# Softmax attention on TensorE: key tiles taken in pairs instead of singly

## The chip, the cores and the metric

One core of a Trainium2 chip runs the whole program. The metric is the device time of one execution in microseconds (us), as a median of several runs. TensorE multiplies, VectorE reduces, ScalarE exponentiates, GpSimd adds, SyncE issues most transfers.

## The reference

Four conditioned blocks follow each other on x of 2 x 2048 rows and 512 columns: a selective scan (Mamba), a softmax attention, and two linear attentions. The change lies in the second alone. Cut to what matters:

```python
def _L1_cond_ref(x, emb, src_mask, ...):
    xn = layer_norm(x, norm_w, norm_b)
    q = (xn @ q_w + q_b).reshape(Bx, Tx, H, -1)      # H = 16 heads of 32
    k = (xn @ k_w + k_b).reshape(Bx, Tx, H, -1)
    att = jnp.einsum('bnhl,bmhl->bnmh', q, k)
    att = att + (1.0 - mask) * -1000000.0
    att = jax.nn.softmax(att, axis=2)                # over the 2048 keys
    v = ((xn @ v_w + v_b) * src_mask[:, :, None]).reshape(Bx, Tx, H, -1)
    y = jnp.einsum('bnmh,bmhl->bnhl', att, v).reshape(Bx, Tx, Dx)
```

With two sequences and 16 heads there are 32 heads of 2048 queries by 2048 keys.

## The kernel before

`stage_attention` is written out by hand: each engine has its own program, the order in it is the order of execution, and engines wait for each other on counting semaphores. Every head is 16 **units** `u`, a unit being one tile of 128 keys against all 2048 queries in `QB` = 4 chunks of 512.

Queries and keys lie stacked (`q_st`, `k_st`; three slots, so three heads are in flight). Each score is computed twice. The **maximum** matmul (`max_mm`) puts 128 queries on the partitions and 512 keys along the bank; VectorE's `reduce` takes the row maximum out of one of three banks (`ps_max`, `BANKS` = 3), and a maximum matmul waits until the bank three items earlier is read (`free_bank`). When all 64 maxima of a head are there, VectorE makes one small tile `m_all`, TensorE turns it (`turn_max`), ScalarE and VectorE split it into two parts (`first_part`, `second_part`), and SyncE writes them as two rows into `q_st` (`max_rows`). The **score** matmul (`score_mm`) then puts 128 keys on the partitions, and the stacked rows subtract the maximum; ScalarE's `exp` empties one of three `ps_s` banks into `prob`, which has `SLOTS` = 4 units.

The **product** (`pv_mm`) multiplies the four chunks of `prob` with the values, as four tiles of 32 columns side by side; each of the four instructions leaves two records in the trace. GpSimd adds the `prob` of the units of a group (`SIZES`, six groups a head) into one of two `pair_sum` buffers, and the **denominator** (`den_mm`) multiplies that sum by ones, again in four column tiles. GpSimd may start a group only when the denominator of the group two earlier is done. `turn_o` turns the finished head's products and denominators back; VectorE's `read_o` inverts and multiplies them.

The maxima run ahead of the scores: during unit u of head hd TensorE makes the maxima of head hd + 1, `LEAD` = 3 units further on, and from unit `TURN_MAX` = 13 those of head hd + 2. During unit u it makes the scores of unit u + 1. `turn_o` follows unit 2, `turn_max` unit 13. The order of a unit on TensorE:

```python
for c in range(QB):
    if u + 1 < QT:
        score_mm(hd, u + 1, c)
    elif hd + 1 < HEADS:
        score_mm(hd + 1, 0, c)
    if tiles:
        max_mm(item_at(hd, "max", u, c), *tiles[c])
pv_mm(hd, u)
```

Of the kernel before, what the change touches and what calls it, by code (L numbers as in the profile page):

```python
# [952 lines left out]
QT = S // P  # L953
# [169 lines left out]
def stage_attention(nc, a, keep, parts, mask_parts, v):  # L1123

    with ExitStack() as ctx:
# [3 lines left out]
        QB = S // CH  # L1129
        NMAX = QT * QB  # L1130
        PER = NMAX // QT
        LEAD = 3
        SIZES = (2, 3, 3, 2, 3, 3)
        GROUPS = [tuple(range(sum(SIZES[:g]), sum(SIZES[:g + 1]))) for g in range(len(SIZES))]
        NGRP = len(GROUPS)
        GROUP_END = {units[-1]: g for g, units in enumerate(GROUPS)}
# [9 lines left out]
        SLOTS = 4  # L1146
        HEADS = NB * H1
        TURN_MAX = QT - LEAD
        TURN_O = 2
        DEN_LAG = 2  # L1150
        q_st = [r.sb(f"q_stack{i}", [ROWS, S], F32R) for i in range(3)]
        k_st = [r.sb(f"k_stack{i}", [ROWS, S], F32R) for i in range(3)]
        prob = [r.sb(f"prob{i}", [P, S]) for i in range(SLOTS)]
# [16 lines left out]
        s = {n: r.sem(n) for n in names.split()}  # L1170
# [4 lines left out]
        def max_tiles(hd, u):  # L1175

            ahead, i = (1, (u + LEAD) * PER) if u < TURN_MAX else (2, (u - TURN_MAX) * PER)
            return [(hd + ahead, i + j) for j in range(PER)] if hd + ahead < HEADS else []

        def bank_items(hd):  # L1180

            items = []
            for u in range(QT):
                items += [("max", u, j) for j in range(len(max_tiles(hd, u)))]
                if u == TURN_O and hd:
                    items.append(("turn_o", u, 0))
                if u == TURN_MAX and hd + 1 < HEADS:
                    items.append(("turn_max", u, 0))
            return items

        BEFORE = NMAX + 1 + LEAD * PER
# [4 lines left out]
        def item_at(hd, kind, u, j=0):  # L1196

            return first_item[hd] + bank_items(hd).index((kind, u, j))
# [57 lines left out]
        @block.tensor  # L1256
        def _(pe):
            def free_bank(seq):
                if seq >= BANKS:
                    pe.wait_ge(s["bank_read"], seq - BANKS + 1)  # L1260
                return ps_max[seq % BANKS]

            def max_mm(seq, hd, i):
                slot = hd % 3
                if i == 0:
                    pe.wait_ge(stack_in[slot], (hd // 3 + 1) * NSTACK * 16)
                qt, kc = divmod(i, QB)
                nc.tensor.matmul(free_bank(seq)[:, :], q_st[slot][0:ROWS_MAX, qt * P:(qt + 1) * P],  # L1268
                                 k_st[slot][0:ROWS_MAX, kc * CH:(kc + 1) * CH], start=True, stop=True).then_inc(s["bank_filled"], 1)

            def turn_max(seq, hd):
                pe.wait_ge(s["m_done"], hd + 1)
                nc.tensor.transpose(free_bank(seq)[0:QT, 0:P], m_all[:, :], keep["ident"][:, :]).then_inc(s["bank_filled"], 1)

            def turn_o(seq, hd):
                pe.wait_ge(s["o_copied"], hd + 1)
                bank = free_bank(seq)
                for t in range(CH // P):
                    mm = nc.tensor.transpose(bank[:, t * P:(t + 1) * P], o_raw[:, t * P:(t + 1) * P], keep["ident"][:, :])
                mm.then_inc(s["bank_filled"], 1)  # L1280
                pe.wait_ge(s["den_copied"], hd + 1)
                for t in range(CH // P):
                    mm = nc.tensor.transpose(ps_d[:, t * P:(t + 1) * P], d_raw[:, t * P:(t + 1) * P], keep["ident"][:, :])
                mm.then_inc(s["den_turned"], 1)

            def score_mm(hd, kt, c):
                n = (hd * QT + kt) * QB + c
                slot = hd % 3
                if kt == 0 and c == 0:
                    pe.wait_ge(s["max_in"], (hd + 1) * 32)  # L1290
                if n >= BANKS:
                    pe.wait_ge(s["exp_done"], n - BANKS + 1)
                nc.tensor.matmul(ps_s[n % BANKS][:, :], k_st[slot][0:ROWS, kt * P:(kt + 1) * P],  # L1293
                                 q_st[slot][0:ROWS, c * CH:(c + 1) * CH], start=True, stop=True).then_inc(s["s_mm"], 1)

            def pv_mm(hd, kt):

                if kt == 0:
                    pe.wait_ge(s["v_copied"], hd + 1)
                    if hd:  # L1300
                        pe.wait_ge(s["o_copied"], hd)
                pe.wait_ge(s["exp_done"], (hd * QT + kt + 1) * QB)
                for c in range(QB):
                    mm = nc.tensor.matmul(ps_o[c * DH1:(c + 1) * DH1, :], v_h[hd % 3][:, kt, :],  # L1304
                                          prob[kt % SLOTS][:, c * CH:(c + 1) * CH], start=(kt == 0), stop=(kt == QT - 1))
                mm.then_inc(s["o_mm"], 1)

            def den_mm(hd, g):

                if g == 0 and hd:  # L1310
                    pe.wait_ge(s["den_read"], hd)
                pe.wait_ge(s["sum_done"], hd * ADDS + sums[g])
                for c in range(QB):
                    mm = nc.tensor.matmul(ps_d[c * DH1:(c + 1) * DH1, :], ones[:, :],
                                          pair_sum[g % 2][:, c * CH:(c + 1) * CH], start=(g == 0), stop=(g == NGRP - 1))
                mm.then_inc(s["den_mm"], 1)

            for i in range(NMAX):
                max_mm(i, 0, i)
            turn_max(NMAX, 0)  # L1320
            for i in range(LEAD * PER):
                max_mm(NMAX + 1 + i, 1, i)
            for c in range(QB):
                score_mm(0, 0, c)
            pe.wait_ge(s["ones_set"], 1)
            for hd in range(HEADS):
                for u in range(QT):
                    tiles = max_tiles(hd, u)
                    for c in range(QB):
                        if u + 1 < QT:  # L1330
                            score_mm(hd, u + 1, c)
                        elif hd + 1 < HEADS:
                            score_mm(hd + 1, 0, c)
                        if tiles:
                            max_mm(item_at(hd, "max", u, c), *tiles[c])
                    pv_mm(hd, u)
                    if u >= DEN_LAG and u - DEN_LAG in GROUP_END:
                        den_mm(hd, GROUP_END[u - DEN_LAG])
                    elif u < DEN_LAG and hd and u - DEN_LAG + QT in GROUP_END:
                        den_mm(hd - 1, GROUP_END[u - DEN_LAG + QT])  # L1340
                    if u == TURN_O and hd:
                        turn_o(item_at(hd, "turn_o", u), hd - 1)
                    if u == TURN_MAX and hd + 1 < HEADS:
                        turn_max(item_at(hd, "turn_max", u), hd + 1)
            den_mm(HEADS - 1, NGRP - 1)
            turn_o(first_item[HEADS], HEADS - 1)

        @block.scalar
        def _(act):
# [23 lines left out]
                nc.scalar.activation(d_raw[:, :], ps_d[:, :], ACT.Copy).then_inc(s["den_copied"], 1)  # L1373

            first_part(NMAX, 0)
            for c in range(QB):
                exp(0, 0, c)
            for hd in range(HEADS):
                for u in range(QT):
                    for c in range(QB):  # L1380
                        if u + 1 < QT:
                            exp(hd, u + 1, c)
                        elif hd + 1 < HEADS:
                            exp(hd + 1, 0, c)
                    if u == TURN_O - 1 and hd:
                        copy_den(hd - 1)
                    if u == TURN_MAX and hd + 1 < HEADS:
                        first_part(item_at(hd, "turn_max", u), hd + 1)
                copy_o(hd)
            copy_den(HEADS - 1)  # L1390

# [1 line left out]
        def _(dve):  # L1393
# [16 lines left out]
            def read_o(seq, hd):  # L1410
                dve.wait_ge(s["den_turned"], hd + 1)
                if hd:
                    dve.wait_ge(s["bank_read"], item_at(hd, "turn_o", TURN_O) + 1)
                nc.vector.reciprocal(rden[:, :].rearrange("p (t c) -> p t c", c=QB),
                                     ps_d[:, :].rearrange("p (t c e) -> p t c e", c=QB, e=DH1)[:, :, :, 0]).then_inc(s["den_inv"], 1)
                dve.wait_ge(s["den_inv"], hd + 1)
# [13 lines left out]
            for i in range(LEAD * PER):  # L1430
                reduce(NMAX + 1 + i, 1, i)
            for hd in range(HEADS):
                for u in range(QT):
                    for j, tile in enumerate(max_tiles(hd, u)):
                        reduce(item_at(hd, "max", u, j), *tile)
                    if u == TURN_O and hd:
                        read_o(item_at(hd, "turn_o", u), hd - 1)
                    if u == TURN_MAX and hd + 1 < HEADS:
                        second_part(item_at(hd, "turn_max", u), hd + 1)
            read_o(first_item[HEADS], HEADS - 1)  # L1440


# [514 lines left out]
```

## Time and profile before

| | us |
|---|---|
| median of 3 runs | 5804.73 (5799.05 to 5807.38) |
| profiled execution, from its first to its last instruction | 5801.9 |
| first maximum matmul of the attention stage begins at | 2525.16 |
| last denominators of the stage begin at | 4347.55 |
| stretch 2632 to 4286: TensorE, VectorE, ScalarE, GpSimd busy | 1653.30, 1221.98, 1021.81, 1415.92 of 1654.00 |

The attention stage is nearly a third of the span. A row of the timeline gives the start, the duration, the engine, the line, the operation and how many were merged (x4); in brackets stands the idle time of the engine before it and what ended it. TensorE's weight loads have rows of their own (PEld). Matmuls overlap, and each lasts longer than the distance to the next: distances are read from starts. The first matmul after a wait or after a change of shape is recorded at its weight load, so the next one stands further away.

### The profile page before, as it was taken

The page shows a single profiled execution, that of the slowest core. Times are in us where ns is not written, and L with a number is a line of the kernel's source. Part 1 is how long each engine was busy: PE and PEld are TensorE (multiplying, and loading weights), DVE is VectorE, ACT ScalarE, POOL GpSimd, SP SyncE. Part 2 cuts the span into 40 slices and gives each one's busy share as a digit, 9 for nine tenths or more (in the row PEclk, how much of TensorE's full clock was granted, in tenths as well). Part 3 has the DMA queues.
Part 4 walks back from the last instruction along what each step waited for, and adds up shares of the span by engine and source line. Part 5 has one row for each costly group of instructions (what it writes and reads, how often), then busy time and mean ns, then how long its engine had stood idle before and what let it go on. Part 6 is the DMA issues. An engine that isn't in the chain of part 4 may idle for free. (4 is left out here: it accounts for less than half of the span.)

```text
span 5801.9 us, 58747 instructions
## 1 busy us (share of the span) xinstructions
PE 5279.5 (91%) x19584; PEld 2503.0 (43%) x19584; DVE 4122.6 (71%) x5430; ACT 2812.6 (48%) x4847; POOL 3279.8 (57%) x2136
## 2 busy tenths in 40 slices
PE   7888989888898879989999999999998889989898
PEld 2333333333333324445455454445544454544545
DVE  6999999999999963267777777777745444445444
ACT  4757566575756523326666666666661121312121
POOL 3879797887979741128888888888880000000000
PEclk9999999999999999979999999999999999999999
DMA  4021211212122023321111111111103202021101
GB/s 167 22 102 66 80 73 51 81 43 102 41 101 77 29 109 124 117 62 34 23 34 34 23 34 23 34 34 23 34 1 134 91 17 69 17 104 35 60 26 51
DMA packets 116735, 346.28 MB, mean 60 GB/s; under 512 B 12272, under 2 KB 13520, under 8 KB 102032
## 3 DMA queue, kind: packets, MB, share of 16 engines
q1 hardware_dynamic: 98512, 294.46, 15.5%
q0 software_dynamic: 9216, 33.56, 1.5%
q10 hardware_dynamic: 8704, 14.50, 0.7%
q8 instruction: 155, 2.54, 0.2%
q14 instruction: 148, 1.21, 0.1%
HBM read 274.29 MB, written 67.67 MB: 59 GB/s over the span
## 5 line engine op out<-in xcount | busy, mean ns | idle before, releaser
L1397 DVE TENSOR_REDUCE attn_mx<-attn_ps_max 128x1 f32<-128x512 f32 x2048 | 1270.1, 683 | 405.0 <-PE attn_ps_max L1268 400.4
L425 POOL TENSOR_TENSOR mamba_hc<-mamba_h,mamba_bc 128x1024 f32<-128x1024 f32 x512 | 1216.8, 2377 | 352.1 <-DVE mamba_h L658 298.2
L1363 ACT ACTIVATE attn_prob<-attn_ps_s 128x512 f32<-128x512 f32 x2048 | 1061.0, 604 | 590.3 <-PE attn_ps_s L1293 587.1
L805 PE MATMUL mamba_y<-mamba_hc,ident 128*128 128x512 f32 x2048 | 1013.0, 618 | 253.6 <-POOL mamba_hc L425 252.7
L1251 POOL TENSOR_TENSOR attn_pair_sum<-attn_prob 128x1024 f32<-128x1024 f32 x384 | 906.6, 2382 | 313.1 <-ACT attn_prob L1363 313.1
L528 ACT ACTIVATE mamba_da<-mamba_dt,mamba_a_neg 128x512 f32<-128x512 f32 x1024 | 689.6, 689 | 686.1 <-DVE mamba_h L658 682.9
L658 DVE TENSOR_TENSOR_SCAN mamba_h<-mamba_da,mamba_state,mamba_h 128x512 f32<-128x512 f32 x768 | 939.7, 1265 | 1.9 <-ACT mamba_da L528 1.9
L1293 PE MATMUL attn_ps_s<-attn_q_stack,attn_k_stack 100*128 100x512 f32 x2048 | 862.1, 424 | 4.2 <-ACT attn_prob L1363 4.2
L1268 PE MATMUL attn_ps_max<-attn_k_stack,attn_q_stack 98*128 98x512 f32 x2048 | 835.9, 415 | 16.8 <-DMA attn_q_stack<-qk_parts 16.1
L805 PEld LDWEIGHTS mamba_y<-mamba_hc,ident 128*128 128x128 f32 x2048 | 374.3, 193 | 836.4 <-POOL mamba_hc L425 422.1
L648 DVE TENSOR_TENSOR mamba_h<-mamba_du,mamba_bc 128x1024 f32<-128x1024 f32 x512 | 619.2, 1209 | 65.6 <-POOL mamba_state L427 57.4
L1251 POOL TENSOR_TENSOR attn_pair_sum<-attn_pair_sum,attn_prob 128x1024 f32<-128x1024 f32 x256 | 604.6, 2384 | 0.0
L1293 PEld LDWEIGHTS attn_ps_s<-attn_q_stack,attn_k_stack 100*128 100x128 f32 x2048 | 387.2, 190 | 455.9 <-ACT attn_prob L1363 232.3
L1304 PE MATMUL attn_ps_o<-attn_prob,attn_v_h 128*32 128x512 f32 x4096 | 546.3, 605 | 0.0
L1268 PEld LDWEIGHTS attn_ps_max<-attn_k_stack,attn_q_stack 98*128 98x128 f32 x2048 | 396.6, 194 | 133.7 <-DVE attn_mx L1397 40.3
L913 POOL TENSOR_TENSOR lin_norm_rstd<-lin_norm_var_eps,neg_half 128x4 f32<-128x4 f32 x16 | 16.1, 1007 | 597.3 <-DVE lin_norm_var_eps L902 597.3
L913 POOL TENSOR_TENSOR lin_out_norm_rstd<-lin_out_norm_var_eps,neg_half 128x4 f32<-128x4 f32 x16 | 16.1, 1006 | 581.1 <-DVE lin_out_norm_var_eps L902 581.1
L658 DVE TENSOR_TENSOR_SCAN mamba_h<-mamba_da,mamba_zeros,mamba_h 128x512 f32<-128x512 f32 x256 | 313.3, 1265 | 0.8 <-ACT mamba_da L528 0.8
L793 PE MATMUL mamba_work<-mamba_w,mamba_zy 128*128 128x512 f32 x512 | 253.9, 623 | 31.6 <-DVE mamba_x_in L676 31.1
L750 PE MATMUL mamba_work<-mamba_xn_t,mamba_w 128*128 128x512 f32 x512 | 249.0, 614 | 1.1 <-ACT mamba_xn_t L463 0.9
L761 PE MATMUL mamba_work<-mamba_xn_t,mamba_w 128*128 128x512 f32 x512 | 242.2, 595 | 0.0
L1646 PE MATMUL lin_mm_bank<-lin_w_q,lin_norm_xn_t 128*128 128x512 f32 x512 | 226.3, 600 | 15.1 <-DVE lin_k_t L1800 15.1
(232 smaller groups left out, 6094.9 us busy)
## 6 DMA issues: line engine op xcount, KB each, us to landing
mamba_bc<-bc_dram SPq DMA_DIRECT2D x64, 1024.0 KB, 7.2
mamba_w<-in_in_proj_w_T SPq DMA_DIRECT2D x16, 2048.0 KB, 7.8
qk_parts<-qkv_pair POOLq DMA_DIRECT2D x64, 512.0 KB
attn_k_stack<-qk_parts SPq DMA_DIRECT2D x96, 256.0 KB
attn_q_stack<-qk_parts SPq DMA_DIRECT2D x96, 256.0 KB
mamba_x_in<-in_x SPq DMA_DIRECT2D x16, 1024.0 KB, 5.3
mamba_w<-in_out_proj_w_T SPq DMA_DIRECT2D x8, 2048.0 KB, 8.3
lin_norm_x<-x_after_L SPq DMA_DIRECT2D x16, 1024.0 KB, 5.7
```

The costliest lines, as they stand in the source:

```text
L425: nc.gpsimd.tensor_tensor(hc[:, gs % HC_SLOTS, :, :], h[:, gs % H_SLOTS, :, :], bc[:, g, G:2 * G, :], ALU.mult).then_inc(s["hc_done"], 1)
L528: nc.scalar.activation(da[n % DA_BANKS][:, :], dt[:, ct % 2, :], ACT.Exp, scale=a_neg[:, ct, g * G + j:g * G + j + 1]).then_inc(s["exp_don ...
L648: nc.vector.tensor_tensor(h[:, gs % H_SLOTS, :, :], du[:, :].unsqueeze(1).to_broadcast([P, G, CH]), bc[:, g, 0:G, :], ALU.mult).then_inc(s ...
L658: nc.vector.tensor_tensor_scan(h[:, gs % H_SLOTS, j, :], da[(gs * G + j) % DA_BANKS][:, :], h[:, gs % H_SLOTS, j, :], first, ALU.mult, ALU ...
L793: mm = nc.tensor.matmul(at("out", it, t)[:, :], zy[:, k, t * P:(t + 1) * P], w_view("out", it)[:, k, :], start=(k == 0), stop=(k == CT - 1))
L805: mm = nc.tensor.matmul(y[ct % 2][:, :], ident[:, :], hc[:, gs % HC_SLOTS, j, :], start=(g == 0 and j == 0), stop=(g == NG - 1 and j == G ...
L1251: nc.gpsimd.tensor_tensor(pair_sum[g % 2][:, at], first[:, at], prob[unit % SLOTS][:, at], ALU.add).then_inc(s["sum_done"], 1)
L1268: nc.tensor.matmul(free_bank(seq)[:, :], q_st[slot][0:ROWS_MAX, qt * P:(qt + 1) * P], k_st[slot][0:ROWS_MAX, kc * CH:(kc + 1) * CH], start ...
L1293: nc.tensor.matmul(ps_s[n % BANKS][:, :], k_st[slot][0:ROWS, kt * P:(kt + 1) * P], q_st[slot][0:ROWS, c * CH:(c + 1) * CH], start=True, st ...
L1304: mm = nc.tensor.matmul(ps_o[c * DH1:(c + 1) * DH1, :], v_h[hd % 3][:, kt, :], prob[kt % SLOTS][:, c * CH:(c + 1) * CH], start=(kt == 0), ...
L1363: nc.scalar.activation(prob[kt % SLOTS][:, c * CH:(c + 1) * CH], ps_s[n % BANKS][:, :], ACT.Exp).then_inc(s["exp_done"], 1)
L1397: nc.vector.tensor_reduce(mx[hd % 3][:, qt, kc:kc + 1], ps_max[seq % BANKS][:, :], AX.X, ALU.max).then_inc(s["bank_read"], 1)
```

## The change

Units are taken in pairs (`UNITS` = 2). In pair p the eight maxima and eight scores of two units alternate, a maximum first; then come both products, then the denominators that are due, then a turn if one is due. Scores run two units ahead instead of one, with as many scores and exps before the loop. `LEAD` goes from 3 to 4, so 16 instead of 12 maxima of head 1 are made before the loop, and `TURN_MAX` from 13 to 12. The groups of the denominators become 3, 3, 2, 3, 3, 2, and each group's denominator goes to the pair that `DEN_AT` names: pairs 2, 3, 4, 6, 7 and the next head's pair 0. `turn_o` follows pair 1, `turn_max` pair 5. ScalarE's and VectorE's programs follow the same order. No instruction is added or removed, and the banks, slots and buffers stay as they are.

```diff
-        LEAD = 3
-        SIZES = (2, 3, 3, 2, 3, 3)
+        LEAD = 4
+        UNITS = 2
+        SIZES = (3, 3, 2, 3, 3, 2)
...
-        TURN_O = 2
+        PAIR_O, PAIR_MAX = 1, TURN_MAX // UNITS - 1
         DEN_LAG = 2
+        DEN_AT = {}
+        for g, units in enumerate(GROUPS):
+            DEN_AT.setdefault(max((units[-1] + DEN_LAG) // UNITS, PAIR_O + 1), []).append(g)
...
-            for c in range(QB):
-                score_mm(0, 0, c)
+            for u in range(UNITS):
+                for c in range(QB):
+                    score_mm(0, u, c)
             pe.wait_ge(s["ones_set"], 1)
             for hd in range(HEADS):
-                for u in range(QT):
-                    tiles = max_tiles(hd, u)
-                    for c in range(QB):
-                        if u + 1 < QT:
-                            score_mm(hd, u + 1, c)
-                        elif hd + 1 < HEADS:
-                            score_mm(hd + 1, 0, c)
-                        if tiles:
-                            max_mm(item_at(hd, "max", u, c), *tiles[c])
-                    pv_mm(hd, u)
-                    if u >= DEN_LAG and u - DEN_LAG in GROUP_END:
-                        den_mm(hd, GROUP_END[u - DEN_LAG])
-                    elif u < DEN_LAG and hd and u - DEN_LAG + QT in GROUP_END:
-                        den_mm(hd - 1, GROUP_END[u - DEN_LAG + QT])
-                    if u == TURN_O and hd:
-                        turn_o(item_at(hd, "turn_o", u), hd - 1)
-                    if u == TURN_MAX and hd + 1 < HEADS:
-                        turn_max(item_at(hd, "turn_max", u), hd + 1)
-            den_mm(HEADS - 1, NGRP - 1)
+                for pair in range(QT // UNITS):
+                    for u in range(pair * UNITS, (pair + 1) * UNITS):
+                        tiles = max_tiles(hd, u)
+                        for c in range(QB):
+                            if tiles:
+                                max_mm(item_at(hd, "max", u, c), *tiles[c])
+                            if u + UNITS < QT:
+                                score_mm(hd, u + UNITS, c)
+                            elif hd + 1 < HEADS:
+                                score_mm(hd + 1, u + UNITS - QT, c)
+                    for u in range(pair * UNITS, (pair + 1) * UNITS):
+                        pv_mm(hd, u)
+                    for g in DEN_AT.get(pair, []):
+                        den_mm(hd, g)
+                    if hd:
+                        for g in DEN_AT.get(pair + QT // UNITS, []):
+                            den_mm(hd - 1, g)
+                    if pair == PAIR_O and hd:
+                        turn_o(item_at(hd, "turn_o", pair), hd - 1)
+                    if pair == PAIR_MAX and hd + 1 < HEADS:
+                        turn_max(item_at(hd, "turn_max", pair), hd + 1)
...
                 for pair in range(QT // UNITS):
                     for u in range(pair * UNITS, (pair + 1) * UNITS):
-                    for c in range(QB):
-                        if u + 1 < QT:
-                            exp(hd, u + 1, c)
-                        elif hd + 1 < HEADS:
-                            exp(hd + 1, 0, c)
-                    if u == TURN_O - 1 and hd:
+                        for c in range(QB):
+                            if u + UNITS < QT:
+                                exp(hd, u + UNITS, c)
+                            elif hd + 1 < HEADS:
+                                exp(hd + 1, u + UNITS - QT, c)
+                    if pair == PAIR_O - 1 and hd:
                         copy_den(hd - 1)
```

TensorE in the middle of a head, before: one unit and the two products around it. `attn_ps_max` is a maximum, `attn_ps_s` a score, `attn_ps_o` a product, `attn_ps_d` a denominator; the numbers are those of the banks and slots.

```order
L1304 MATMUL attn_ps_o<-attn_prob0,attn_v_h0 32x512 x4
L1293 MATMUL attn_ps_s0<-attn_q_stack0,attn_k_stack0 128x512
L1268 MATMUL attn_ps_max1<-attn_k_stack1,attn_q_stack1 128x512
L1293 MATMUL attn_ps_s1<-attn_q_stack0,attn_k_stack0 128x512
L1268 MATMUL attn_ps_max2<-attn_k_stack1,attn_q_stack1 128x512
L1293 MATMUL attn_ps_s2<-attn_q_stack0,attn_k_stack0 128x512
L1268 MATMUL attn_ps_max0<-attn_k_stack1,attn_q_stack1 128x512
L1293 MATMUL attn_ps_s0<-attn_q_stack0,attn_k_stack0 128x512
L1268 MATMUL attn_ps_max1<-attn_k_stack1,attn_q_stack1 128x512
L1304 MATMUL attn_ps_o<-attn_prob1,attn_v_h0 32x512 x4
```

TensorE in the middle of a head, now: the end of one block of sixteen, what follows it, and the first half of the next block.

```order
L1298 MATMUL attn_ps_s0<-attn_q_stack0,attn_k_stack0 128x512
L1309 MATMUL attn_ps_o<-attn_prob0,attn_v_h0 32x512 x4
L1309 MATMUL attn_ps_o<-attn_prob1,attn_v_h0 32x512 x4
L1319 MATMUL attn_ps_d<-attn_pair_sum1,attn_ones 32x512 x4
L1273 MATMUL attn_ps_max1<-attn_k_stack1,attn_q_stack1 128x512
L1298 MATMUL attn_ps_s1<-attn_q_stack0,attn_k_stack0 128x512
L1273 MATMUL attn_ps_max2<-attn_k_stack1,attn_q_stack1 128x512
L1298 MATMUL attn_ps_s2<-attn_q_stack0,attn_k_stack0 128x512
L1273 MATMUL attn_ps_max0<-attn_k_stack1,attn_q_stack1 128x512
L1298 MATMUL attn_ps_s0<-attn_q_stack0,attn_k_stack0 128x512
L1273 MATMUL attn_ps_max1<-attn_k_stack1,attn_q_stack1 128x512
L1298 MATMUL attn_ps_s1<-attn_q_stack0,attn_k_stack0 128x512
```

Eight maxima now stand between two groups of products where four stood, and the second product stands directly behind the first.

VectorE over one head, before, from the small tile of a head's maxima (`attn_m_all`) on:

```order
L1400 TENSOR_REDUCE attn_m_all<-attn_mx 128x16
L1397 TENSOR_REDUCE attn_mx<-attn_ps_max 128x1 x4
L1404 SCALAR_TENSOR_TENSOR attn_m_parts<-attn_ps_max,attn_m_parts 16x128
L1397 TENSOR_REDUCE attn_mx<-attn_ps_max 128x1 x20
L1414 RECIPROCAL attn_rden<-attn_ps_d 128x16
L1419 TENSOR_TENSOR v<-attn_ps_max,attn_rden 128x4x4x32
```

VectorE over one head, now:

```order
L1413 TENSOR_REDUCE attn_m_all<-attn_mx 128x16
L1417 SCALAR_TENSOR_TENSOR attn_m_parts<-attn_ps_max,attn_m_parts 16x128
L1410 TENSOR_REDUCE attn_mx<-attn_ps_max 128x1 x32
L1427 RECIPROCAL attn_rden<-attn_ps_d 128x16
L1432 TENSOR_TENSOR v<-attn_ps_max,attn_rden 128x4x4x32
```

The four reductions that stood between `attn_m_all` and the split of the maxima are gone from there, so `turn_max` follows the last maxima of its head at once.

## Rows read from the trace of the kernel before

**Rows 1.** The page's first line: the span.
```profile
span 5801.9 us, 58747 instructions
```

**Rows 2.** Busy time by stretch: sum, then engines, TensorE's clock, DMA share, GB/s.
```profile
core 0: us, PE busy (x) PEld busy (x) DVE busy (x) ACT busy (x) POOL busy (x), PEclk, DMA share, GB/s
2632.00:4286.00 1654.00, 1653.30 (x9316) 827.72 (x9315) 1221.98 (x2022) 1021.81 (x1992) 1415.92 (x625) 1.00 0.13 28
```

**Rows 3.** Timeline of TensorE, one unit and the next: start, duration, operation.
```profile
3299.65 1.07 PE L1304 MATMUL attn_ps_o<-attn_prob,attn_v_h 128*32 128x512 f32 x8
3300.65 0.50 PE L1293 MATMUL attn_ps_s<-attn_q_stack,attn_k_stack 100*128 100x512 f32 x1
3300.99 0.39 PE L1268 MATMUL attn_ps_max<-attn_k_stack,attn_q_stack 98*128 98x512 f32 x1
...
3302.40 0.39 PE L1268 MATMUL attn_ps_max<-attn_k_stack,attn_q_stack 98*128 98x512 f32 x1
3302.72 1.07 PE L1304 MATMUL attn_ps_o<-attn_prob,attn_v_h 128*32 128x512 f32 x8
3303.60 1.04 PE L1314 MATMUL attn_ps_d<-attn_pair_sum,attn_ones 128*32 128x512 f32 x8
3304.57 0.50 PE L1293 MATMUL attn_ps_s<-attn_q_stack,attn_k_stack 100*128 100x512 f32 x1
```

**Rows 4.** Timeline of TensorE in the last heads, to the last denominators.
```profile
4284.73 0.50 PE L1293 MATMUL attn_ps_s<-attn_q_stack,attn_k_stack 100*128 100x512 f32 x1
...
4287.80 0.98 PE L1293 MATMUL attn_ps_s<-attn_q_stack,attn_k_stack 100*128 100x512 f32 x3
4288.99 0.50 PE L1293 MATMUL attn_ps_s<-attn_q_stack,attn_k_stack 100*128 100x512 f32 x1 [0.21 <-ACT attn_prob L1363]
...
4340.88 1.04 PE L1314 MATMUL attn_ps_d<-attn_pair_sum,attn_ones 128*32 128x512 f32 x8
4341.74 1.04 PE L1304 MATMUL attn_ps_o<-attn_prob,attn_v_h 128*32 128x512 f32 x8
4347.55 1.94 PE L1314 MATMUL attn_ps_d<-attn_pair_sum,attn_ones 128*32 128x512 f32 x8 [4.77 <-POOL attn_pair_sum L1251]
```

**Rows 5.** VectorE's reductions: the page's group, then two rows of its timeline.
```profile
L1397 DVE TENSOR_REDUCE attn_mx<-attn_ps_max 128x1 f32<-128x512 f32 x2048 | 1270.1, 683 | 405.0 <-PE attn_ps_max L1268 400.4
...
2525.99 38.35 DVE L1397 TENSOR_REDUCE attn_mx<-attn_ps_max 128x1 f32<-128x512 f32 x64 [1.87 <-PE attn_ps_max L1268]
...
3301.42 2.48 DVE L1397 TENSOR_REDUCE attn_mx<-attn_ps_max 128x1 f32<-128x512 f32 x4 [0.58 <-PE attn_ps_max L1268]
```

**Rows 6.** Timeline of all engines after `turn_o`.
```profile
3308.48 0.51 PE L1293 MATMUL attn_ps_s<-attn_q_stack,attn_k_stack 100*128 100x512 f32 x1
...
3309.77 2.47 DVE L1397 TENSOR_REDUCE attn_mx<-attn_ps_max 128x1 f32<-128x512 f32 x4
...
3310.51 0.19 PEld L1268 LDWEIGHTS attn_ps_max<-attn_k_stack,attn_q_stack 98*128 98x128 f32 x1 [0.30 <-DVE attn_mx L1397]
...
3310.94 1.07 PE L1304 MATMUL attn_ps_o<-attn_prob,attn_v_h 128*32 128x512 f32 x8
...
3315.87 0.50 PE L1293 MATMUL attn_ps_s<-attn_q_stack,attn_k_stack 100*128 100x512 f32 x1
```

**Rows 7.** Timelines of TensorE and VectorE after `turn_max`.
```profile
3346.03 0.28 PE L1273 MATMUL attn_ps_max<-ident,attn_m_all 128*16 128x128 f32 x1
...
3347.07 2.49 DVE L1397 TENSOR_REDUCE attn_mx<-attn_ps_max 128x1 f32<-128x512 f32 x4
...
3353.15 0.50 PE L1293 MATMUL attn_ps_s<-attn_q_stack,attn_k_stack 100*128 100x512 f32 x1
```

**Rows 8.** Waits from 2576 to 4280 us: us in total, times, longest.
```profile
PEld attn_ps_max L1268 <- DVE attn_mx L1397: 18.0, 60, 0.3
```

**Rows 9.** Timelines of ScalarE (one unit's exps) and GpSimd (two adds).
```profile
3301.19 2.07 ACT L1363 ACTIVATE attn_prob<-attn_ps_s 128x512 f32<-128x512 f32 x4 [0.91 <-PE attn_ps_s L1293]
...
3317.63 4.72 POOL L1251 TENSOR_TENSOR attn_pair_sum<-attn_prob 128x1024 f32<-128x1024 f32 x2 [1.81 <-ACT attn_prob L1363]
```

More of the change, by code:

```diff
@@ L1182, in bank_items @@
             items = []
-            for u in range(QT):
-                items += [("max", u, j) for j in range(len(max_tiles(hd, u)))]
-                if u == TURN_O and hd:
-                    items.append(("turn_o", u, 0))
-                if u == TURN_MAX and hd + 1 < HEADS:
-                    items.append(("turn_max", u, 0))
+            for pair in range(QT // UNITS):
+                for u in range(pair * UNITS, (pair + 1) * UNITS):
+                    items += [("max", u, j) for j in range(len(max_tiles(hd, u)))]
+                if pair == PAIR_O and hd:
+                    items.append(("turn_o", pair, 0))
+                if pair == PAIR_MAX and hd + 1 < HEADS:
+                    items.append(("turn_max", pair, 0))
             return items
@@ L1322, in _ @@
                 max_mm(NMAX + 1 + i, 1, i)
-            for c in range(QB):
-                score_mm(0, 0, c)
+            for u in range(UNITS):
+                for c in range(QB):
+                    score_mm(0, u, c)
             pe.wait_ge(s["ones_set"], 1)
             for hd in range(HEADS):
-                for u in range(QT):
-                    tiles = max_tiles(hd, u)
-                    for c in range(QB):
-                        if u + 1 < QT:
-                            score_mm(hd, u + 1, c)
-                        elif hd + 1 < HEADS:
-                            score_mm(hd + 1, 0, c)
-                        if tiles:
-                            max_mm(item_at(hd, "max", u, c), *tiles[c])
-                    pv_mm(hd, u)
-                    if u >= DEN_LAG and u - DEN_LAG in GROUP_END:
-                        den_mm(hd, GROUP_END[u - DEN_LAG])
-                    elif u < DEN_LAG and hd and u - DEN_LAG + QT in GROUP_END:
-                        den_mm(hd - 1, GROUP_END[u - DEN_LAG + QT])
-                    if u == TURN_O and hd:
-                        turn_o(item_at(hd, "turn_o", u), hd - 1)
-                    if u == TURN_MAX and hd + 1 < HEADS:
-                        turn_max(item_at(hd, "turn_max", u), hd + 1)
@@ L1345, in _ @@
-            den_mm(HEADS - 1, NGRP - 1)
+                for pair in range(QT // UNITS):
+                    for u in range(pair * UNITS, (pair + 1) * UNITS):
[7 more added lines that the diff above has]
+                                score_mm(hd + 1, u + UNITS - QT, c)
+                    for u in range(pair * UNITS, (pair + 1) * UNITS):
+                        pv_mm(hd, u)
[4 more added lines that the diff above has]
+                            den_mm(hd - 1, g)
+                    if pair == PAIR_O and hd:
+                        turn_o(item_at(hd, "turn_o", pair), hd - 1)
+                    if pair == PAIR_MAX and hd + 1 < HEADS:
+                        turn_max(item_at(hd, "turn_max", pair), hd + 1)
@@ L1346, in _ @@
+            for at in range(QT // UNITS, max(DEN_AT) + 1):
+                for g in DEN_AT.get(at, []):
+                    den_mm(HEADS - 1, g)
             turn_o(first_item[HEADS], HEADS - 1)
@@ L1375, in _ @@
             first_part(NMAX, 0)
-            for c in range(QB):
-                exp(0, 0, c)
+            for u in range(UNITS):
+                for c in range(QB):
+                    exp(0, u, c)
             for hd in range(HEADS):
-                for u in range(QT):
-                    for c in range(QB):
-                        if u + 1 < QT:
-                            exp(hd, u + 1, c)
-                        elif hd + 1 < HEADS:
-                            exp(hd + 1, 0, c)
-                    if u == TURN_O - 1 and hd:
+                for pair in range(QT // UNITS):
+                    for u in range(pair * UNITS, (pair + 1) * UNITS):
+                        for c in range(QB):
+                            if u + UNITS < QT:
[3 more added lines that the diff above has]
+                    if pair == PAIR_O - 1 and hd:
                         copy_den(hd - 1)
-                    if u == TURN_MAX and hd + 1 < HEADS:
-                        first_part(item_at(hd, "turn_max", u), hd + 1)
+                    if pair == PAIR_MAX and hd + 1 < HEADS:
+                        first_part(item_at(hd, "turn_max", pair), hd + 1)
                 copy_o(hd)
@@ L1412, in read_o @@
                 if hd:
-                    dve.wait_ge(s["bank_read"], item_at(hd, "turn_o", TURN_O) + 1)
+                    dve.wait_ge(s["bank_read"], item_at(hd, "turn_o", PAIR_O) + 1)
                 nc.vector.reciprocal(rden[:, :].rearrange("p (t c) -> p t c", c=QB),
@@ L1432, in _ @@
             for hd in range(HEADS):
[L1433 to L1439, printed above, removed]
+                for pair in range(QT // UNITS):
+                    for u in range(pair * UNITS, (pair + 1) * UNITS):
+                        for j, tile in enumerate(max_tiles(hd, u)):
+                            reduce(item_at(hd, "max", u, j), *tile)
+                    if pair == PAIR_O and hd:
+                        read_o(item_at(hd, "turn_o", pair), hd - 1)
+                    if pair == PAIR_MAX and hd + 1 < HEADS:
+                        second_part(item_at(hd, "turn_max", pair), hd + 1)
             read_o(first_item[HEADS], HEADS - 1)
```

## The prediction

> **What bounds the kernel now.** I read the page's first lines for the span, 5801.9 us [rows 1], then the busy time by stretch: from 2632 to 4286 us, inside the attention stage, TensorE is busy 1653.30 of 1654.00 us at a granted clock of 1.00, the 2.4 GHz level [rows 2]. A busy TensorE need not stream at its best, so I went on to the timeline of one unit.
>
> A unit begins with eight full-width matmuls (scores and maxima in turn, here a "full block") and ends with the four column-tiled products with the values (PV, eight records). Products start 3299.65 and 3302.72: a unit takes 3.07 us [rows 3]. Inside a full block one matmul follows another at (3302.40 - 3300.99)/6 = 0.235 us. Three places are slower: from the first matmul of a block to the second 0.34, from the last to PV 0.32, from PV to the next block 1.00. From PV to a denominator group (den), also column-tiled, it is only 0.88, and from den to the block 0.97 [rows 3]; a PV that follows a den starts 0.86 after it [rows 4]. So going to tiles and back costs (0.32 - 0.235) + (0.97 - 0.86) + (0.34 - 0.235) = 0.30 us, once in every unit. 0.34 + 6 x 0.235 + 0.32 + 1.00 = 3.07 leaves nothing else: the unit is bound by TensorE, its switches included.
>
> VectorE reduces a maximum bank in 683 ns [rows 5], and back to back one each (38.35 - 0.68)/63 = 0.598 us [rows 5]. That is slower than TensorE fills them, one each 0.47 us. With four in a row, then a PV, three banks hide it: in 1704 us the weight loads of the maxima wait for VectorE 60 times, two a head, 18.0 us in all [rows 8].
>
> **What the change removes.** Two units now share one block of sixteen, then PV, PV, and den where there is one. Sixteen: 0.34 + 14 x 0.235 + 0.32 = 3.95 from its first matmul to PV. PV to the next column-tiled group 0.88. The step PV to PV is not in the trace; I take the 0.88 of PV to den, its nearest row [rows 3]. Its lower end is 0.86 (den to PV) [rows 4], its upper end 1.00 (as if it switched). The last PV, which now follows a tiled group, leaves for the next block after 0.97. Together 5.80 us against 2 x 3.07 = 6.14: a gain of 0.34 for a pair, if nothing waits.
>
> **What takes its place: eight maxima in a row through three banks.** Count from the block's first matmul, now a maximum. A matmul in stream is reduced 0.43 after its start (3300.99 to 3301.42) [rows 3, 5], one that starts a block 0.11 later, so the first reduction begins at 0.54, and those after it at 0.54 + 0.598 n. Maximum n (from 0) may load when reduction n - 3 has ended; the trace shows that load 0.06 after the end (3309.77 + 0.68 to 3310.51) [rows 6]. The eighth, n = 7, waits for reduction 4: 0.54 + 4 x 0.598 + 0.68 + 0.06 = 3.67. After a late load the next matmul follows by 0.34, as at a block's start, and PV by 0.32: PV at 4.33 rather than 3.95. That is a stall of 0.385, and the first four maxima cause none of it. A pair then takes 4.33 + 0.88 + 0.97 = 6.18, 0.045 **more** than now. A den adds 0.86 before and after (3.92 for a unit with one against 3.07).
>
> **The two turns cost more.** After `turn_o` VectorE must invert and multiply before it reduces; its first reduction begins 1.29 after the block does (3308.48 to 3309.77) [rows 6]. Today that costs 0.39 (PV 2.46 after the block's start instead of 2.07), because only four maxima follow. In a block of sixteen the eighth loads at 1.29 + 4 x 0.598 + 0.74 = 4.42, PV at 5.08, and the pair with its den takes 5.08 + 0.88 + 0.86 + 0.97 = 7.79. Before, the same two units took 3315.87 - 3308.48 = 7.39: +0.40. After `turn_max` the first reduction begins 1.04 after the turn (3346.03 to 3347.07) [rows 7]: PV at 1.04 + 2.39 + 0.74 + 0.66 = 4.83, the pair with its den 7.54, before 3353.15 - 3346.03 = 7.12: +0.42. `turn_max` itself now follows directly on the last maxima. Its input is ready at 0.54 + 7 x 0.598 + 0.68 plus about 0.3 for the small reduction, 5.7, and TensorE gets there at 4.33 + 0.88 + 0.97 = 6.18: no wait, with 0.5 to spare.
>
> **Edits I cost at nothing.** Eight exps at (2.07 - 0.60)/3 = 0.49 [rows 9] follow scores at 0.47; the eighth score needs exp 4, ended at 0.78 + 4 x 0.49 + 0.60 = 3.3, before it is due. If the exps were slower than about 0.57 they would replace VectorE as the wait. The new `SIZES` leave GpSimd twenty adds a head at 2.36 (two in 4.72) [rows 9], 47 of some 56 us. A group's first add waits for the den two groups earlier, which frees its buffer at the end of a pair; the exp that needs that add stands at the start of the pair after next, 7.0 + 0.8 us later, and the add takes 4.7: 3 us to spare. The transfers of the maximum rows are issued on SyncE just after `turn_max`, at the start of pair 6, and needed by the scores of pair 7. VectorE's queue waits in `read_o` with its pair's maxima already done.
>
> **The edges.** Four more reductions before the loop (4 x 0.60) and four more exps (4 x 0.49): +4.4. At the end, from 4284.73 to the last den at 4347.55 [rows 4], 62.8 us: without maxima, exps pace the scores (the fourth starts 1.19 after the first [rows 4], so the eighth 1.19 + 4 x 0.49 = 3.15, a pair 5.4). Two such pairs with den, 12.6, then GpSimd's ten double adds of the last head with their waits, about 49: 61.7, so -1. Bounds -4 and +2. Edges +3.4.
>
> **The sum.** Pairs with maxima: 30 heads x 8, and 6 of head 30: 246. 30 follow `turn_o`, 30 `turn_max`, 186 neither. 186 x 0.045 = 8.4; 30 x 0.40 = 12.0; 30 x 0.42 = 12.6; edges 3.4: **+36 us**. On the profiled span that is 5838; the median of the runs is 2.8 us above it, so 5804.7 + 36 = 5841.
>
> **A rule that points the other way.** The trace shows 0.30 us for each round trip to tiles [rows 3, 4]. The Trainium skill (TensorEngine Tiling (Array Packing), Key Properties) says that changing the tiling mode drains TensorE; halving the changes is then a plain gain, the first rival below. The same page (PSUM Bottleneck) says that tiling speeds up TensorE but not the emptying of PSUM, so that this may become the limit; taken as a mean rate it would not be one here, and the sum would stay at that rival's. Neither sentence knows of the three banks.
>
> **Rivals.** With a stall of s in each pair the whole is 246 x (s - 0.34) + 22 (what the turns add, 60 x 0.37) + 3.4.
> 1. *Faster: the switches go and nothing comes back.* By mean rates VectorE needs 8 x 0.598 = 4.8 of 5.8 us, so if the banks' wait did not reach TensorE the gain would be 246 x 0.34 = 84, less the edges: 5724. For it: the two waits a head today. Against: those two are just where VectorE starts late by 0.5 us and more, and before the loop 64 reductions follow each other at 0.598 without a gap [rows 5]. It turns faster at s under 0.19, a reduction each 0.55 us instead of 0.598. Chance 0.10.
> 2. *No difference.* s between 0.19 and 0.28, a reduction each 0.55 to 0.57, or starting 0.1 to 0.2 us sooner than I count: 5805. Chance 0.12.
> 3. *Much slower: the second PV opens the tiles anew*, 1.00 rather than 0.88, so the change does not do what it says: 256 x 0.12 = 31 more, 5872. Against it: den after PV, the same shapes, pays no switch [rows 3]. Chance 0.08.
>
> **How the numbers follow.** The forecast, 5841, has 0.70. Its unknowns: 0.03 on the stall and the steps moves 186 to 246 pairs by 6 to 8 us, the turns 0.1 x 60 = 6, the edges 3: 5820 to 5860. The range 5806 to 5872 takes in the upper half of rival 2 and reaches rival 3; rival 1 and the rest stay out. About 0.2%, 11.6 us, is what a measurement of this kernel can tell from no change. Slower by more: 0.70 + 0.08 = 0.78; within: 0.12; faster: 0.10.
>
> **What the next profile would show.** Right: maxima waiting for VectorE some three times a pair, over 700 times and about 0.25 us each, the last block matmul to PV still 0.32, a plain pair of 6.1 to 6.25 us, PV to PV 0.86 to 0.88, VectorE without gaps inside a block. Wrong: pairs of 5.8 us with few such waits (rival 1); PV to PV of 1.00 (rival 3); or exps waiting for GpSimd, which would break the claim of 3 us to spare.

## The result and the profile after

The changed kernel takes 5841.39 us (median of 4 runs, 5840.75 to 5844.16) against 5804.83 for the kernel before in the same comparison: 1.0069 times as long, 95% interval 1.0056 to 1.0081. The forecast was 5841 us, in a range from 5806 to 5872.

The page after begins with the new span, and VectorE's reductions have not become slower; they answer to [rows 1, 5].

```profile
span 5839.7 us, 58747 instructions
...
L1410 DVE TENSOR_REDUCE attn_mx<-attn_ps_max 128x1 f32<-128x512 f32 x2048 | 1247.2, 681 | 411.8 <-PE attn_ps_max L1273 407.4
```

The waits of the stage after (2576 to 4310 us; total, times, longest) answer to [rows 8].

```profile
PEld attn_ps_max L1273 <- DVE attn_mx L1410: 293.3, 1034, 0.8
...
POOL attn_pair_sum L1256 <- PE attn_ps_d L1319: 278.1, 121, 3.2
...
PEld attn_ps_d L1319 <- POOL attn_pair_sum L1256: 0.6, 2, 0.3
```

Weight loads of the maxima now wait for VectorE 1034 times, before 60 times. In the whole list no exp waits for GpSimd, and TensorE waits for GpSimd's sums twice, for 0.6 us in all: the claim of 3 us to spare held. GpSimd does wait for denominators, as the two sum buffers make it, and nobody waits for that.

A plain pair with its denominators, from the timeline after (start, duration, engine, operation). It answers to [rows 3]:

```profile
3309.39 0.50 PE L1273 MATMUL attn_ps_max<-attn_k_stack,attn_q_stack 98*128 98x512 f32 x1
...
3309.93 4.87 DVE L1410 TENSOR_REDUCE attn_mx<-attn_ps_max 128x1 f32<-128x512 f32 x8 [2.18 <-PE attn_ps_max L1273]
...
3311.28 0.19 PEld L1273 LDWEIGHTS attn_ps_max<-attn_k_stack,attn_q_stack 98*128 98x128 f32 x1 [0.17 <-DVE attn_mx L1410]
3311.87 0.19 PEld L1273 LDWEIGHTS attn_ps_max<-attn_k_stack,attn_q_stack 98*128 98x128 f32 x1 [0.30 <-DVE attn_mx L1410]
3312.47 0.19 PEld L1273 LDWEIGHTS attn_ps_max<-attn_k_stack,attn_q_stack 98*128 98x128 f32 x1 [0.30 <-DVE attn_mx L1410]
3313.07 0.19 PEld L1273 LDWEIGHTS attn_ps_max<-attn_k_stack,attn_q_stack 98*128 98x128 f32 x1 [0.30 <-DVE attn_mx L1410]
3313.41 0.40 PE L1298 MATMUL attn_ps_s<-attn_q_stack,attn_k_stack 100*128 100x512 f32 x1
3313.74 1.92 PE L1309 MATMUL attn_ps_o<-attn_prob,attn_v_h 128*32 128x512 f32 x16
3315.49 1.04 PE L1319 MATMUL attn_ps_d<-attn_pair_sum,attn_ones 128*32 128x512 f32 x8
3316.46 0.50 PE L1273 MATMUL attn_ps_max<-attn_k_stack,attn_q_stack 98*128 98x512 f32 x1
```

VectorE starts 0.54 after the block and reduces eight banks without a gap. The eighth maximum loads 3.68 after the block's start and the products begin at 4.35; the two products take 1.75, the denominators 0.97, the pair 7.07, which is 6.21 without the 0.86 of the denominators. The steps had 3.67, 4.33, 1.74, 0.97, 7.04 and 6.18. The late loads stand one reduction (0.598) apart: 3311.28, 3311.87, 3312.47, 3313.07. From the last matmul of the block to the products it is 0.33 (3313.41 to 3313.74; 0.32 before), so the lateness comes from inside the block.

After the turns, from the timelines of TensorE and VectorE; these answer to [rows 7] and [rows 6]:

```profile
3301.84 0.28 PE L1278 MATMUL attn_ps_max<-ident,attn_m_all 128*16 128x128 f32 x1
...
3302.88 4.88 DVE L1410 TENSOR_REDUCE attn_mx<-attn_ps_max 128x1 f32<-128x512 f32 x8
...
3306.68 1.92 PE L1309 MATMUL attn_ps_o<-attn_prob,attn_v_h 128*32 128x512 f32 x16
...
3330.54 0.48 PE L1273 MATMUL attn_ps_max<-attn_k_stack,attn_q_stack 98*128 98x512 f32 x1
...
3331.84 4.87 DVE L1410 TENSOR_REDUCE attn_mx<-attn_ps_max 128x1 f32<-128x512 f32 x8
...
3335.63 1.92 PE L1309 MATMUL attn_ps_o<-attn_prob,attn_v_h 128*32 128x512 f32 x16
...
3338.34 0.50 PE L1273 MATMUL attn_ps_max<-attn_k_stack,attn_q_stack 98*128 98x512 f32 x1
```

From `turn_max` to the products 4.84, and 7.55 to the next pair (3309.39); after `turn_o` 5.09, and 7.80. The steps had 4.83 and 7.54, 5.08 and 7.79.

### The profile page after: what moved, and what is told of

Same layout as the page of the kernel before. It is cut to its first block and busy times, and to the rows that moved or that the text cites. A ratio compares the mean times of both kernels' runs of the same rounds, so it can differ in the third digit from the quotient of the medians.

```text
span 5839.7 us, 58747 instructions
## 1 busy us (share of the span) xinstructions
PE 5293.7 (91%) x19584; PEld 2452.7 (42%) x19584; DVE 4098.3 (70%) x5430; ACT 2872.3 (49%) x4847; POOL 3281.8 (56%) x2136
## 5 line engine op out<-in xcount | busy, mean ns | idle before, releaser
L1410 DVE TENSOR_REDUCE attn_mx<-attn_ps_max 128x1 f32<-128x512 f32 x2048 | 1247.2, 681 | 411.8 <-PE attn_ps_max L1273 407.4
L1374 ACT ACTIVATE attn_prob<-attn_ps_s 128x512 f32<-128x512 f32 x2048 | 1110.7, 603 | 505.1 <-PE attn_ps_s L1298 502.1
L805 PE MATMUL mamba_y<-mamba_hc,ident 128*128 128x512 f32 x2048 | 997.9, 610 | 271.7 <-POOL mamba_hc L425 269.5
L1273 PE MATMUL attn_ps_max<-attn_k_stack,attn_q_stack 98*128 98x512 f32 x2048 | 949.3, 471 | 24.9 <-DMA attn_q_stack<-qk_parts 15.8
L1298 PE MATMUL attn_ps_s<-attn_q_stack,attn_k_stack 100*128 100x512 f32 x2048 | 815.2, 400 | 2.1 <-ACT attn_prob L1374 2.1
L1309 PE MATMUL attn_ps_o<-attn_prob,attn_v_h 128*32 128x512 f32 x4096 | 492.4, 598 | 0.0
```

What stands on the lines that cost most here:

```text
L805: mm = nc.tensor.matmul(y[ct % 2][:, :], ident[:, :], hc[:, gs % HC_SLOTS, j, :], start=(g == 0 and j == 0), stop=(g == NG - 1 and j == G ...
L1374: nc.scalar.activation(prob[kt % SLOTS][:, c * CH:(c + 1) * CH], ps_s[n % BANKS][:, :], ACT.Exp).then_inc(s["exp_done"], 1)
L1410: nc.vector.tensor_reduce(mx[hd % 3][:, qt, kc:kc + 1], ps_max[seq % BANKS][:, :], AX.X, ALU.max).then_inc(s["bank_read"], 1)
```

## The experiments

The theory: the change saves about 0.34 us of tile switches in a pair, and loses 0.385 because eight maxima in a row go through three banks that VectorE empties at 0.598 us each. The rivals: the longer block or the second product is slow by itself; the saving was never there; the lead or the groups cost the time.

### Take the suspected wait away

Each reduction reads half of its bank, in the changed kernel (`e1_half_after`) and, as a control, in the kernel before (`e2_half_before`).

```diff
-                nc.vector.tensor_reduce(mx[hd % 3][:, qt, kc:kc + 1], ps_max[seq % BANKS][:, :], AX.X, ALU.max).then_inc(s["bank_read"], 1)
+                nc.vector.tensor_reduce(mx[hd % 3][:, qt, kc:kc + 1], ps_max[seq % BANKS][:, 0:CH // 2], AX.X, ALU.max).then_inc(s["bank_read"], 1)
```

> The changed kernel, but each reduction of a maximum bank reads 256 of its 512 columns (the maxima then miss half of the keys). Theory (three banks and a reduction each 0.598 us make the block of sixteen stall by 0.385 us): a reduction comes down to about 0.33 us each, below the 0.47 of the maxima, the stall goes, a pair without denominators takes 5.80 us instead of 6.18. Pairs 186 x -0.34, pairs after the turns 60 x -0.22 against the kernel before, the 80 maxima before the loop about 14 us faster: near 5719 (5705 to 5740). Rival, the longer block or the second product is what costs: the pair stays at 6.1 or more, and only the 14 us before the loop go: 5827.

> Control: the kernel before with the same halved reductions. Theory: its units wait for VectorE only twice a head, so it gains the 13 us before the loop and a few at the turns: 5787 (5780 to 5795), and the changed kernel with halved reductions is about 68 us faster than this one. Rival, VectorE holds the kernel before as well: 5750 or less, and no difference between the two halved kernels is left.

Measured: 5705.91 us, 0.9833 (0.982 to 0.9847) of the kernel before, and for the control 5774.98, 0.9952 (0.9939 to 0.9966). TensorE's timeline of the halved changed kernel:

```profile
3301.43 0.50 PE L1273 MATMUL attn_ps_max<-attn_k_stack,attn_q_stack 98*128 98x512 f32 x1
...
3305.37 1.92 PE L1309 MATMUL attn_ps_o<-attn_prob,attn_v_h 128*32 128x512 f32 x16
3307.11 1.04 PE L1319 MATMUL attn_ps_d<-attn_pair_sum,attn_ones 128*32 128x512 f32 x8
3308.08 0.50 PE L1273 MATMUL attn_ps_max<-attn_k_stack,attn_q_stack 98*128 98x512 f32 x1
```

and its waits of maxima for VectorE's reductions, from 2576 to 4300 us:

```profile
PEld attn_ps_max L1273 <- DVE attn_mx L1410: 6.9, 30, 0.6
```

The products begin 3.94 after the block's start, where an unstalled block was reckoned at 3.95, and a pair with denominators takes 6.65 (5.80 + 0.86 = 6.66). The 1034 waits have become 30. So the saving of the switches is real, and with the wait gone it arrives: the halved changed kernel is 69.1 us faster than the halved kernel before, where 68 was expected, while with whole reductions the changed one is 36.6 us slower. That is a swing of 106 us on one cause.

Both halved kernels came out about 12 us lower than the middle of what was expected, and the control below its range of 5780 to 5795. The thirty heads of the loop can be read by themselves, from the first `turn_max` in the loop to the last (the halved changed kernel, then the halved kernel before):

```profile
2599.45 0.28 PE L1278 MATMUL attn_ps_max<-ident,attn_m_all 128*16 128x128 f32 x1
...
4188.78 0.28 PE L1278 MATMUL attn_ps_max<-ident,attn_m_all 128*16 128x128 f32 x1
```

```profile
2609.01 0.28 PE L1273 MATMUL attn_ps_max<-ident,attn_m_all 128*16 128x128 f32 x1
...
4266.95 0.28 PE L1273 MATMUL attn_ps_max<-ident,attn_m_all 128*16 128x128 f32 x1
```

1589.33 us against 1657.94: the pairs and turns alone make a difference of 68.6 us, and it is this that the theory rests on. In the control these heads gained 9.3 us on those of the kernel before (1667.26), more than the few that were reckoned for the turns, and the stretch from the first maximum to the first of these turns gained 15.0 instead of 13. Another 5.0 us of its profile lie behind the attention stage, which the edit does not touch; why is open.

### Make the suspected wait worse

`e3_two_banks_after`: two banks for the maxima.

```diff
-        BANKS = 3
+        BANKS, MBANKS = 3, 2
...
-                if seq >= BANKS:
-                    pe.wait_ge(s["bank_read"], seq - BANKS + 1)
-                return ps_max[seq % BANKS]
+                if seq >= MBANKS:
+                    pe.wait_ge(s["bank_read"], seq - MBANKS + 1)
+                return ps_max[seq % MBANKS]
...
```

> The changed kernel with two banks for the maxima instead of three, nothing else. Theory: maximum n then waits for reduction n - 2, and a bank comes back 1.28 us after it was filled, so two banks give one reduction each 0.64 us; worked out in the same way, the eighth maximum loads 4.45 us after the block's start and the products begin at 5.11 instead of 4.33: 246 x 0.78 = 192 us slower than with three, 6033 (6010 to 6065). Rival, the banks are not what the block waits for: within 20 us of 5841.

Measured: 6049.27 us, 1.0428 (1.0412 to 1.0444), 208 us above the changed kernel. TensorE's timeline:

```profile
3310.20 0.50 PE L1273 MATMUL attn_ps_max<-attn_k_stack,attn_q_stack 98*128 98x512 f32 x1
...
3314.65 0.50 PE L1273 MATMUL attn_ps_max<-attn_k_stack,attn_q_stack 98*128 98x512 f32 x1
...
3315.32 1.92 PE L1309 MATMUL attn_ps_o<-attn_prob,attn_v_h 128*32 128x512 f32 x16
```

The eighth maximum starts 4.45 after the block and the products 5.12 (expected 4.45 and 5.11). The number of banks is what the block waits by. Of the 208 us some 189 lie in the thirty heads; the stretch before the loop grew by 20 more, which the expectation had left out. More banks than three were not tried.

### Put the switch back

`e7_extra_switch`: the last score of a block stands between the two products, so a pair goes to tiles twice; all else is the changed kernel.

```diff
...
                     for u in range(pair * UNITS, (pair + 1) * UNITS):
                         pv_mm(hd, u)
+                        if u % UNITS == 0 and last:
+                            score_mm(*last)
```

> The changed kernel, but the last score of each block of sixteen stands between the two products, so that TensorE goes to tiles and back twice in a pair as the kernel before does, with pairs, lead and groups unchanged. Theory (each round trip costs TensorE 0.30 us): the first product begins 4.10 us after the block's start, the score 1.00 later, the second product 0.42 later, the next block 1.00 later: a pair takes 6.52 instead of 6.18, 250 x 0.34 = 84 us more than the changed kernel, 5925 (5905 to 5945). Rival, the two products back to back save nothing: within 15 us of 5841.

Measured: 5924.16 us, 1.0213 (1.0198 to 1.0229), 83 us above the changed kernel where 84 was expected. TensorE's timeline of a pair with denominators:

```profile
3314.39 0.50 PE L1273 MATMUL attn_ps_max<-attn_k_stack,attn_q_stack 98*128 98x512 f32 x1
...
3318.49 1.06 PE L1309 MATMUL attn_ps_o<-attn_prob,attn_v_h 128*32 128x512 f32 x8
3319.49 0.49 PE L1298 MATMUL attn_ps_s<-attn_q_stack,attn_k_stack 100*128 100x512 f32 x1
3319.91 1.06 PE L1309 MATMUL attn_ps_o<-attn_prob,attn_v_h 128*32 128x512 f32 x8
3320.80 1.04 PE L1319 MATMUL attn_ps_d<-attn_pair_sum,attn_ones 128*32 128x512 f32 x8
3321.77 0.50 PE L1273 MATMUL attn_ps_max<-attn_k_stack,attn_q_stack 98*128 98x512 f32 x1
```

The first product begins at 4.10, since the last score no longer stands ahead of it; from there to the second product it takes 1.00 + 0.42 instead of some 0.88, and the pair takes 7.38 (6.52 + 0.86, as reckoned) instead of 7.07. Products back to back do save a round trip.

### The numbers of the change alone

`e8_params_before`: the kernel before with the lead and the groups of the change.

```diff
-        LEAD = 3
-        SIZES = (2, 3, 3, 2, 3, 3)
+        LEAD = 4
+        SIZES = (3, 3, 2, 3, 3, 2)
```

> The kernel before with the numbers of the change alone: maxima lead by four and groups of 3, 3, 2, 3, 3, 2, units taken singly. Theory: neither bears on TensorE's path in the loop; four more maxima before the loop cost 2.4 us and come off later at less: 5806 (5797 to 5815). Rival, the lead or the groups make up a good part of the 37 us: 5820 or more.

Measured: 5802.87 us, 1.0003 (0.9994 to 1.0011). Neither number carries any part of the 37 us that could be measured.

### A block order that lets the late maxima be late

`e4_order`: the same sixteen matmuls, ordered so that the last scores stand ahead of the last maxima.

```diff
-                        for c in range(QB):
-                            if tiles:
-                                max_mm(item_at(hd, "max", u, c), *tiles[c])
-                            if u + UNITS < QT:
-                                score_mm(hd, u + UNITS, c)
...
+                    for kind in "msmsmsmsmssmsmsm":
+                        u, c = next(maxima if kind == "m" else scores)
...
```

> The changed kernel with another order inside the block of sixteen on TensorE: m s m s m s m s m s s m s m s m, so that the last three maxima stand later and the last scores in front of them; nothing else. Theory: the eighth maximum still loads 3.67 us after the block's start, but nothing of the block follows it, so the products begin at 3.67 + 0.11 + 0.32 = 4.10 instead of 4.33: 246 x -0.23 = -56, 5785 (5775 to 5800), faster than both kernels. Rival, the time is lost somewhere else than behind the last maxima: no change, 5841; a second rival, the exps now hold the late scores up: slower than 5841.

Measured: 5782.01 us, 0.9967 (0.9954 to 0.9979): 59 us below the changed kernel and faster than the kernel before. TensorE's timeline:

```profile
3313.51 0.50 PE L1273 MATMUL attn_ps_max<-attn_k_stack,attn_q_stack 98*128 98x512 f32 x1
...
3317.23 0.45 PE L1273 MATMUL attn_ps_max<-attn_k_stack,attn_q_stack 98*128 98x512 f32 x1
3317.61 1.92 PE L1309 MATMUL attn_ps_o<-attn_prob,attn_v_h 128*32 128x512 f32 x16
3319.35 1.04 PE L1319 MATMUL attn_ps_d<-attn_pair_sum,attn_ones 128*32 128x512 f32 x8
3320.32 0.50 PE L1273 MATMUL attn_ps_max<-attn_k_stack,attn_q_stack 98*128 98x512 f32 x1
```

The products begin at 4.10 as reckoned, and the pair takes 6.81.

### The turn ahead of the products

`e5_order_turn` is that order with `turn_o` ahead of pair 1's products (denominators turned first); `e6_turn_before` makes the same edit alone, in the kernel before.

```diff
+                    if pair == PAIR_O and hd:
+                        turn_o(item_at(hd, "turn_o", pair), hd - 1)
                     for u in range(pair * UNITS, (pair + 1) * UNITS):
                         pv_mm(hd, u)
...
-                    if pair == PAIR_O and hd:
-                        turn_o(item_at(hd, "turn_o", pair), hd - 1)
```

> The block order m s m s m s m s m s s m s m s m, and the turn of the finished head placed ahead of the products of pair 1 instead of behind them (denominators turned first). Theory: VectorE then inverts and multiplies while TensorE makes the two products, the first reduction of pair 2 begins 0.54 us after its block instead of 1.29, and 30 pairs lose their extra 0.75 us: 22 us less than with the block order alone, near 5763 (5750 to 5780). Rival, the turn only moves its wait to pair 1 (its bank is free when reduction 5 ends, 4.2 us after the block's start): no gain over the block order alone.

> The kernel before with one edit, the turn of the finished head ahead of the product of unit 2 instead of behind it (denominators turned first). Theory: the 0.39 us by which the unit after the turn is late goes in 31 heads: -12 us, 5793. Rival, the wait moves to the product: no change, 5805.

Measured: 5762.89 us, 0.9934 (0.992 to 0.9947), 19 us below the order alone and the fastest of all kernels that compute the whole; and 5791.06, 0.9984 (0.9975 to 0.9992), 11 us below the kernel before. VectorE's timeline of `e5_order_turn` around that turn:

```profile
3344.70 4.87 DVE L1413 TENSOR_REDUCE attn_mx<-attn_ps_max 128x1 f32<-128x512 f32 x8 [1.94 <-PE attn_ps_max L1273]
3349.50 0.24 DVE L1430 RECIPROCAL attn_rden<-attn_ps_d 128x16 f32<-128x16 f32 x1
3349.89 0.69 DVE L1435 TENSOR_TENSOR v<-attn_ps_max,attn_rden 128x512 f32<-128x512 f32 x1
3351.55 4.87 DVE L1413 TENSOR_REDUCE attn_mx<-attn_ps_max 128x1 f32<-128x512 f32 x8 [0.97 <-PE attn_ps_max L1273]
```

VectorE does the turn's work in what was idle time and then still waits 0.97 us for the next maximum: the extra lateness of that pair is gone.

## Why the prediction was right, point by point

**TensorE and its switches bound the unit.** Right: a pair without the wait takes 6.65, reckoned 5.80 and its 0.86 (`e1_half_after`), and a switch put back costs 83 us, reckoned 84 (`e7_extra_switch`).

**PV to PV, taken as 0.88.** Right: both products take 1.74 to 1.75 to the next column-tiled group, that is 0.88 + 0.86. Rival 3's 1.00 would have made it 1.86.

**The stall of 0.385 from three banks.** Right in place and size: products at 4.35 instead of 3.95, and the runs with less and with more of the wait move the time as reckoned. Rival 1's saving exists: it arrived when the reductions were made shorter than the distance of the maxima (`e1_half_after`), and in part with another order (`e4_order`). One detail was off: I expected three waits a pair, and there are four. The first of them (0.17, at 3311.28) costs TensorE nothing, since its load would have stood idle until the matmul ahead of it had streamed.

**The turns.** Right: 7.80 and 7.55 against 7.79 and 7.54.

**The sum.** Right at +36 against +36.6 measured, but two terms were off by some 3 to 5 us each, and that they cancelled was luck. The head goes from turn to turn, by the first and the last `turn_max` inside the loop (before, then after; thirty heads each):

```profile
2623.16 0.28 PE L1273 MATMUL attn_ps_max<-ident,attn_m_all 128*16 128x128 f32 x1
...
4290.42 0.28 PE L1273 MATMUL attn_ps_max<-ident,attn_m_all 128*16 128x128 f32 x1
```

```profile
2620.15 0.28 PE L1278 MATMUL attn_ps_max<-ident,attn_m_all 128*16 128x128 f32 x1
...
4324.84 0.28 PE L1278 MATMUL attn_ps_max<-ident,attn_m_all 128*16 128x128 f32 x1
```

1667.26 us against 1704.69: +37.4, or 1.25 a head. The steps gave 6 x 0.045 + 0.40 + 0.42 = 1.09. A plain pair costs about 0.065 to 0.07 instead of 0.045: two units of the kernel before take 6.13 on most rows, not 6.14, and a plain pair after 7.05 to 7.07 with denominators, not 7.04. In a difference of two nearly equal numbers a hundredth of a microsecond counts 186 times. The edges make up for it. The stage as a whole goes from its first maximum to its last denominators:

```profile
2526.45 38.24 PE L1273 MATMUL attn_ps_max<-attn_k_stack,attn_q_stack 98*128 98x512 f32 x64 [15.76 <-DMA attn_q_stack<-qk_parts]
...
4386.21 1.07 PE L1319 MATMUL attn_ps_d<-attn_pair_sum,attn_ones 128*32 128x512 f32 x8 [2.94 <-POOL attn_pair_sum L1256]
```

It took 1859.8 us against 1822.4 before and so grew by 37.4 too; the edges came to about nothing instead of +3.4. The end took 61.4 us from the last `turn_max` (4324.84) instead of 62.8, a gain of 1.4 where 1 was reckoned, so the extra maxima and exps at the start cost less than 4.4.

**The rule that pointed the other way.** A change of tiling has its price: one more round trip made the pair 0.31 us longer in `e7_extra_switch`. The Trainium skill (TensorEngine Tiling (Array Packing), Key Properties) says that such a change drains TensorE; this trace agrees that it costs time, and no row shows what the time goes into. Counting the saved switches alone, the change would have been 84 us faster, less the edges. VectorE is idle for some 2.2 us of each pair of 7.07, so its mean rate was not the limit, but how far three banks let it lag. The Trainium skill (TensorEngine Tiling (Array Packing), PSUM Bottleneck) says that the emptying of PSUM may become the limit once tiling has sped TensorE up; here the late loads, each behind 0.30 us of idle time that a reduction ended, show it as the limit inside a block, though not as a mean rate.

## What to carry to other kernels

An engine that is idle nearly a third of the time can still set the pace, if the work for it comes in bursts longer than its buffers absorb; reckon the burst, item by item, with the number of banks, not the mean rate. When two groups are merged to save a switch, put the items of the slow consumer early in the group and its latest ones at the very end, with the work that depends on nothing ahead of them: here this turned +0.7% into -0.3%, and moving the turn's work into the idle time made it -0.7%.

## What the runs showed of the hardware that was not expected

TensorE's clock before the loop. The same 64 maxima with halved reductions ran at two clocks in two kernels whose programs agree up to there. Their rows, and the busy time by stretch from 2540 to 2549 us, of the halved changed kernel and then of the halved kernel before (the number after the engines is the granted clock):

```profile
2525.30 23.70 PE L1273 MATMUL attn_ps_max<-attn_k_stack,attn_q_stack 98*128 98x512 f32 x64 [16.04 <-DMA attn_q_stack<-qk_parts]
...
2540.00:2549.00 9.00, 9.00 (x27) 4.84 (x26) 9.00 (x27) 0.00 (x0) 0.00 (x0) 1.00 0.00 0
```

```profile
2526.04 28.33 PE L1268 MATMUL attn_ps_max<-attn_k_stack,attn_q_stack 98*128 98x512 f32 x64 [16.04 <-DMA attn_q_stack<-qk_parts]
...
2540.00:2549.00 9.00, 9.00 (x22) 6.00 (x21) 8.76 (x21) 0.00 (x0) 0.00 (x0) 0.50 0.00 1
```

In the first the clock is at 2.4 GHz (1.00), in the second at 1.2 (0.50), with TensorE shown as busy all the time in both, and in both after the same 16.04 us of idle time ahead of the first maximum. With whole reductions it stayed at 0.50 in this stretch in the profiles of both kernels. What set the two apart was not tried. The 64 maxima took 23.70 us in the first, where the granted clock was 0.77 from 2527 to 2540 us, and 28.33 in the second, where it was 0.50; so 4.6 us between the two halved kernels came from here and not from the pairs. From 2590 us on, ahead of the thirty heads, the granted clock was 1.00 in all four profiles.
